# First stage: context loads issued by SP's queue, weights, products and constants by POOL's

## The chip, the cores and the metric

The kernel runs on one core of a Trainium2 chip. The metric is the device time of one execution in microseconds. The engines are PE (matrix products), DVE (VectorE), ACT (ScalarE), POOL (GpSimd) and SP (which here only issues DMAs). A DMA is issued by an engine in its program order: a DMA that has to wait for something holds up all that stands behind it on the same engine. SP's DMAs go through queue q1 (hardware_dynamic), POOL's through q0 (software_dynamic), ACT's few through q10. All three share the core's 16 DMA engines.

## The reference

The input is x (8 x 64 x 512), a context (8 x 1601 x 512) and a mask. Six blocks follow each other, each one added to x after a layer norm. Only the first one matters here; it is a slot attention, repeated three times with the same weights:

```python
Pn = rmsnorm(P, input_norm_w)                 # P: the context
k_proj = Pn @ Wk.T
v_proj = Pn @ Wv.T
for _ in range(NUM_ITERS):                    # 3
    sn = rmsnorm(slots, slot_norm_w)
    q_proj = sn @ Wq.T
    scores = jnp.einsum('bkd,bmd->bkm', q_proj, k_proj) * SCALE
    attn = jax.nn.softmax(scores, axis=-2)
    attn = attn / (jnp.sum(attn, axis=-1, keepdims=True) + EPS)
    updates = jnp.einsum('bkm,bmd->bkd', attn, v_proj)
    slots = gru_cell(updates, slots, gru_wih, gru_whh, gru_bih, gru_bhh)
```

The second block is a state space scan, a product and a feed-forward layer. Its scan is computed as a convolution whose response is a sum over powers of the decay: y_j = sum over n of C B A^j.

## The kernel before

The first stage (about 0 to 802 us) never forms k_proj and v_proj. It multiplies the weights instead: G = Wq^T Wk (`product`, line 489), and Wv with the three input matrices of the recurrent cell (`merged`, line 478). Queries go through G and are then compared with the raw context. G and the three products are stored to HBM once and reloaded in the second and third pass. The products are what the change calls s1.G and s1.m0 to s1.m2.

In each of the three passes the 8 batch rows are done in four pairs. For each pair the contexts of both rows are read anew from HBM, transposed (`transposed`, line 411: 1536 and 1792 KB for the two halves of a row, from rows of 3 and 3.5 KB) and natural (`natural`, line 416: as many bytes, in rows of 2 KB a token that lie behind each other, 12 and 14 KB for row 0 of the pair). A pass moves 54 MB of them. The transposed contexts of a pair go into RA and RB, the natural ones into RC and parts of T and PR; each place is loaded again as soon as the matmuls that read it are done, which is what the waits in `s1_pool` say: `S{h}.{b}` (scores of half h of pair b), `U{h}.{b}` (updates).

After the four pairs comes the recurrent cell with six tiles of weights, whh0, wih0, whh2, wih2, whh1, wih1 in this order (`GRU`, line 391), each 48 matmuls (about 11 us). ACT makes a rounded high part of each tile (`high`), DVE the rest (`low`, line 887), and PE multiplies with both. The tiles come through a ring of 4 slots: SP walks through the list `order` and loads each tile when the one before it in its slot is used (`before[name] + ".used"`), so whh1 waits for whh0 to be used and wih1 for wih0. For the later stages SP goes on with the same list.

POOL issues the context loads of the stage. Then it waits for the last pair's turned updates, issues the load of the mask (line 2064) and computes the powers, 64 dependent multiplications on tiles of 128 x 64 (`s2_pool`, lines 1070 and 1073):

```python
pool.wait_ge(*at.done("s2.decay"))
pool.tensor_tensor(pw[:, 0], abc[:, 1], abc[:, 2], ALU.mult).then_inc(*at.step())
for j in range(1, S):
    pool.wait_ge(*at.own())
    pool.tensor_tensor(pw[:, j], pw[:, j - 1], abc[:, 0], ALU.mult).then_inc(*at.step("s2.powers"))
```

DVE sums them (`response_dve`, line 782) inside the third pass's recurrent cell, after the low parts of the fourth tile (wih2) and ahead of the gate products (L929) and of the low part of the fifth (whh1). ACT makes 48 diagonal tiles of the response (L777) between its tanh and its last sigmoids.

In the first pass there is more: the layer norm of x (L494, L317 on PE), G (L489), the sums of squares of the contexts (L642 on ACT, L801 on DVE), and the merged products (L478).

Of the kernel before, what the change touches and what calls it, by code (L numbers as in the profile page):

```python
# [11 lines left out]
P = 128  # L12
# [12 lines left out]
RING = 4  # L25
# [109 lines left out]

def sem_names():
    return (["tensor_done", "scalar_done", "vector_done", "pool_done", "x_loaded", "consts_loaded", "G_stored", "merged_stored0", "merged_stored1", "merged_stored2", "mask_loaded", "out_stored"]
            + [f"weights_loaded{s}" for s in range(RING)]
            + [f"spare_loaded{s}" for s in range(4)]
            + [f"ctxT_loaded{u}{h}" for u in (0, 1) for h in (0, 1)] + [f"ctxN_loaded{u}{h}" for u in (0, 1) for h in (0, 1)])  # L140


def build(nc, marks, new, t, stages=(1, 2, 3, 4, 5, 6)):
    ctx = ExitStack()
    with ctx:
        address = {}

        def sb(name, shape, dt=FP32):
            address[name] = nc.sbuf_base
            return ctx.enter_context(nc.sbuf_tensor(name, shape, dt))  # L150

        def part(name, of, k=0, n=D):
# [5 lines left out]
        ring = [sb(f"ring{s}", [P, KC, D]) for s in range(RING)]  # L158
        RA, RB, RC = (sb(n, [P, MT * D]) for n in ("RA", "RB", "RC"))
        n0 = HALF[0][1]  # L160
        CT = [RA[:, 0:KC * n0 * P].rearrange("p (c m) -> p c m", c=KC),
              RA[:, KC * n0 * P:KC * MP].rearrange("p (c m) -> p c m", c=KC)]
# [8 lines left out]
        rows = sb("rows", [P, NROW])  # L171
        gw = sb("gw", [P, 2, KC, E_])
# [5 lines left out]
        misc = sb("misc", [P, 512])  # L178
# [24 lines left out]
        scratch = [nc.dram_tensor(f"merged{k}", (P, KC, D), FP32).ap() for k in range(4)]  # L203
# [7 lines left out]
        def row(name, n):  # L211
            return rows[:, RAT[name]:RAT[name] + n]

        sems = {n: ctx.enter_context(nc.semaphore(n)) for n in sem_names()}
        block = ctx.enter_context(nc.Block())

# [6 lines left out]
        order = []  # L223
# [15 lines left out]
        slot, before, place = {}, {}, 0  # L239
# [167 lines left out]
                 [pair(SN, 0), pair(SN, 1), pair(SN, 2), pair(UP, 3)],  # L407
                 [pair(SN, 0), pair(SN, 1), pair(SN, 2), pair(SN, 3)]]

        def s1_pool(pool, at):  # L410
            def transposed(L, b, u, h):
                m0, mt = HALF[h]
                pool.dma_start(CT1[u][h][:, :, :], t["ctxT"][b * 2 + u, :, :, m0 * P:(m0 + mt) * P])\
                    .then_inc(*at.load(f"ctxT_loaded{u}{h}", f"{L}.ct{h}.{u}.{b}"))

            def natural(L, b, u, h):
                m0, mt = HALF[h]
                if u == 0:
                    pool.dma_start(CN0[:, m0:m0 + mt, :], t["ctxN"][b * 2, :, m0:m0 + mt, :])\
                        .then_inc(*at.load(f"ctxN_loaded{u}{h}", f"{L}.cn{h}.{u}.{b}"))  # L420
                    return
                for k, c0, c1 in ((3, 0, 4), (4, 0, 2)) if h == 0 else ((4, 2, 4), (5, 0, 4)):
                    m = 4 * (k - 3)
                    pool.dma_start(TS[k][:, c0:c1, :], t["ctxN"][b * 2 + 1, :, m + c0:m + c1, :])\
                        .then_inc(*at.load(f"ctxN_loaded{u}{h}", f"{L}.cn{h}.{u}.{b}"))
                if h:
                    pool.dma_start(CN1[MT - 1], t["ctxN"][b * 2 + 1, :, MT - 1, :])\
                        .then_inc(*at.load(f"ctxN_loaded{u}{h}", f"{L}.cn{h}.{u}.{b}"))

            for h in (0, 1):  # L430
                for u in (0, 1):
                    natural("s1.0", 0, u, h)
            for h in (0, 1):
                for u in (0, 1):
                    transposed("s1.0", 0, u, h)
            for it in range(3):
                L, N = f"s1.{it}", f"s1.{it + 1}"
                for b in range(PAIRS - 1):
                    for h in (0, 1):
                        pool.wait_ge(*at.done(f"{L}.S{h}.{b}"))  # L440
                        for u in (0, 1):
                            transposed(L, b + 1, u, h)
                    if b:
                        for h in (0, 1):
                            pool.wait_ge(*at.done(f"{L}.U{h}.{b - 1}"))
                            for u in (0, 1):
                                natural(L, b, u, h)
                if it < 2:
                    for h in (0, 1):
                        pool.wait_ge(*at.done(f"{L}.S{h}.{PAIRS - 1}"))  # L450
                        transposed(N, 0, 1, h)
                for h in (0, 1):
                    pool.wait_ge(*at.done(f"{L}.U{h}.{PAIRS - 2}"))
                    for u in (0, 1):
                        natural(L, PAIRS - 1, u, h)
                if it == 2:
                    continue
                for h in (0, 1):
                    pool.wait_ge(*at.done(f"{L}.U{h}.{PAIRS - 1}"))
                    natural(N, 0, 0, h)  # L460
                pool.wait_ge(*at.done(f"{L}.z.3"))
                for h in (0, 1):
                    transposed(N, 0, 0, h)
                pool.wait_ge(*at.done(f"{L}.sl"))
                for h in (0, 1):
                    natural(N, 0, 1, h)

        def s1_pe(pe, at):
            def merged(g):
# [588 lines left out]
        abc = misc[:, 256:448].rearrange("p (a c n) -> p a c n", a=3, c=KC)  # L1058
# [431 lines left out]
        def s4_pool(pool, at):  # L1490
            if 3 in stages:
                pool.wait_ge(*at.done("s3.x5"))
            pool.memset(KT[:, :, n0 * P + M1:MP], 0.0).then_inc(*at.step("s4.pad"))
            for b in range(B):
                N, L = f"s4.{b}", f"s4.{b - 1}"
                m0, mt = HALF[0]
                if b:
                    pool.wait_ge(*at.done(f"{L}.V0"))
                pool.dma_start(CT[0][:, :, :], t["ctxT"][b, :, :, 0:mt * P]).then_inc(*at.load("ctxT_loaded00", f"{N}.ct0"))
                pool.wait_ge(*at.done(f"{N}.ct0"))  # L1500
                if b == 0:
                    pool.wait_ge(*at.done("s4.ln.done"))
                pool.tensor_copy(CH[0][:, :, :], CT[0][:, :, :]).then_inc(*at.step(f"{N}.high0"))
                pool.wait_ge(*at.own())
                pool.tensor_tensor(CL[0][:, :, :], CT[0][:, :, :], CH[0][:, :, :].bitcast(FP32), ALU.subtract).then_inc(*at.step(f"{N}.low0"))

                m0, mt = HALF[1]
                if b:
                    pool.wait_ge(*at.done(f"{L}.t{BLOCKS - 1}"))
                pool.dma_start(CT[1][:, :, :], t["ctxT"][b, :, :, m0 * P:(m0 + mt) * P]).then_inc(*at.load("ctxT_loaded01", f"{N}.ct1"))  # L1510

        def s4_pe(pe, at):
            norm_pe(pe, at, "s4.ln", X, chunk_steps("x3.") if 3 in stages else ["x"])
# [495 lines left out]
        def _(sync):  # L2009
            at = Steps(sems, "out_stored", marks, new)  # L2010

            for dst, src in ((X[:, :, :], t["x"]), (sq[:, :, :], t["squares"]), (vec[:, :], t["vecs"])):
                sync.dma_start(dst, src).then_inc(*at.load("x_loaded", "x"))
            for name, tile in order:
                if tile == "made":
                    for dst, src in ((rows[:, :], t["rows"]), (gw[:, :, :, :], t["gates"]), (misc[:, 256:448].rearrange("p (a b) -> p a b", a=3), t["abc"])):
                        sync.dma_start(dst, src).then_inc(*at.load("consts_loaded", "consts"))
                    at.same("abc", "consts")
                    continue
                if tile is not None:  # L2020
                    if before[name]:
                        sync.wait_ge(*at.done(before[name] + ".used"))
                    if before[name] == "s1.0.G":
                        sync.wait_ge(*at.done("s1.G.stored"))
                    source = t["tiles"][tile] if isinstance(tile, int) else scratch[("s1.G", "s1.m0", "s1.m1", "s1.m2").index(tile)]
                    if not isinstance(tile, int):
                        sync.wait_ge(*at.done(f"{tile}.stored"))
                    sync.dma_start(ring[slot[name]][:, :, :], source).then_inc(*at.load(f"weights_loaded{slot[name]}", name))
                    continue
                if name == "s3.moe":  # L2030
                    for x in before[name]:
# [147 lines left out]
```

## Time and profile before

| | |
|---|---|
| median of 3 runs | 3310.79 us (3310.77 to 3312.28) |
| the profiled execution | 3310.42 us, its span 3308.6 us |
| PE busy | 2950.1 us, 89% |
| DVE, ACT, POOL busy | 1337.6, 1025.8, 268.0 us |
| q1 (SP) | 190.57 MB, 15.2% of 16 engines |
| q0 (POOL) | 192.23 MB, 14.8% |
| DMA share in 0 to 40, 40 to 100, 100 to 200, 200 to 400, 400 to 600, 600 to 800 us | 0.97, 0.86, 0.63, 0.49, 0.72, 0.62 |

The span is what the profiler saw from the first to the last instruction. Busy time is no measure of what a change is worth: what counts is which wait ends last at each place, and the chain of waits shows that.

### The profile page before, as it was taken

How to read it: one execution, taken by the hardware profiler on the slowest of the kernel's cores; microseconds unless marked ns; L12 is line 12 of the kernel's file. 1: busy time of each engine (PE TensorE's matmuls, PEld its weight loads, DVE VectorE, ACT ScalarE, POOL GpSimd, SP SyncE). 2: the span in 40 equal slices, each digit the busy share in tenths (PEclk: the TensorE clock that was granted, in tenths of full speed). 3: DMA queues.
4: the chain of work that ended last, by engine and by line, in shares of the span. 5: the costliest groups of instructions: out<-in, count | busy, mean ns of one | idle time of the engine just before them, and what ended most of it. 6: DMA issues, size and time to landing. Idle time of an engine off the chain costs nothing.

```text
span 3308.6 us, 35885 instructions
## 1 busy us (share of the span) xinstructions
PE 2950.1 (89%) x14622; PEld 2016.9 (61%) x14622; DVE 1337.6 (40%) x2005; ACT 1025.8 (31%) x1717; POOL 268.0 (8%) x274
## 2 busy tenths in 40 slices
PE   7766889888878879999999988999999999988787
PEld 3324537345555347888888857778777877844432
DVE  3435454454842243333333352442443344245211
ACT  3223212224331234433434322422332333233200
POOL 1110120122010000000000002011011101000000
PEclk9887999999889978999999999999999999998899
DMA  8663693861011002222222221001100100021097
GB/s 358 263 241 130 241 412 122 352 267 72 1 52 63 38 13 102 101 93 97 101 89 101 93 78 42 23 20 42 42 23 20 42 23 20 23 108 39 26 419 304
DMA packets 62267, 388.74 MB, mean 117 GB/s; under 512 B 5696, under 2 KB 12096, under 8 KB 32704
## 3 DMA queue, kind: packets, MB, share of 16 engines
q1 hardware_dynamic: 26640, 190.57, 15.2%
q0 software_dynamic: 29024, 192.23, 14.8%
q10 hardware_dynamic: 6480, 4.20, 0.4%
q8 instruction: 91, 1.49, 0.2%
q14 instruction: 32, 0.26, 0.0%
HBM read 381.72 MB, written 5.24 MB: 117 GB/s over the span
## 4 chain that ended last, share of the span: by engine, by line
PE 76%; DVE 7%; DMA 6%; ACT 5%; issue 4%; POOL 2%; SPq 0%; DVEq 0%; POOLq 0%; ACTq 0%
PE PS L373 10%; PE PS L375 10%; PE PS L374 10%; PE PS L544 4%; PE PS L296 4%; PE PS L1571 4%; PE PS L519 3%; PE PS L1552 3%; PE PS L1535 3%; PE PS L1554 3%; PE PS L1553 3%; PE PS L1537 3%; PE PS L1536 3%; DMA PR<-in_ctxN 3%; DMA ring<-in_experts 2%
## 5 line engine op out<-in xcount | busy, mean ns | idle before, releaser
L373 PE MATMUL PS<-X_high,W_high 128*128 128x512 f32 x576 | 226.1, 392 | 27.6 <-POOL W_part L1029 27.6
L374 PE MATMUL PS<-X_low,W_high 128*128 128x512 f32 x576 | 225.6, 392 | 0.0
L375 PE MATMUL PS<-X_high,W_part 128*128 128x512 f32 x576 | 225.5, 391 | 0.0
L375 PE MATMUL PS<-H_high,W_part 128*128 128x512 f32 x576 | 224.4, 390 | 0.0
L374 PE MATMUL PS<-H_low,W_high 128*128 128x512 f32 x576 | 224.4, 390 | 0.0
L373 PE MATMUL PS<-H_high,W_high 128*128 128x512 f32 x576 | 224.4, 390 | 0.0
L1037 DVE TENSOR_TENSOR W_part<-ring,W_high 128x2048 fp32r<-128x2048 f32 x63 | 147.0, 2334 | 188.6 <-ACT W_high L1004 188.6
L1004 ACT ACTIVATE W_high<-ring 128x2048 fp32r<-128x2048 f32 x72 | 136.9, 1914 | 255.0 <-PE PS L375 255.0
L1735 DVE TENSOR_TENSOR RB<-PS,rows 128x512 f32<-128x512 f32 x104 | 71.9, 691 | 307.2 <-PE PS L1554 307.2
L1043 DVE TENSOR_TENSOR H_low<-T,H_high 128x512 fp32r<-128x512 f32 x144 | 99.7, 692 | 221.2 <-ACT H_high L1024 221.2
L1535 PE MATMUL PS<-C_high,W_part 128*128 128x384 f32 (+2 forms) x512 | 177.7, 347 | 4.9 <-DVE W_part L1707 4.9
L1665 ACT ACTIVATE RC<-PS,vec 128x384 f32<-128x384 f32 (+2 forms) x128 | 76.2, 595 | 326.9 <-PE PS L1537 326.9
L1537 PE MATMUL PS<-C_high,W_part 128*128 128x384 f32 (+2 forms) x512 | 176.5, 345 | 0.0
L1536 PE MATMUL PS<-C_low,W_part 128*128 128x384 f32 (+2 forms) x512 | 176.5, 345 | 0.0
L544 PE MATMUL PS<-RC,PTs 128*64 128x512 f32 x312 | 144.7, 622 | 31.1 <-DVE PTs L871 23.4
L1552 PE MATMUL PS<-W_part,C_high 128*128 128x512 f32 x416 | 164.9, 396 | 0.0
L1553 PE MATMUL PS<-W_part,C_high 128*128 128x512 f32 x416 | 162.3, 390 | 0.0
L1554 PE MATMUL PS<-W_part,C_low 128*128 128x512 f32 x416 | 162.3, 390 | 0.0
L519 PE MATMUL PS<-RA,PR 128*64 128x448 f32 (+1 forms) x384 | 145.3, 538 | 18.5 <-DMA RB<-in_ctxT 8.2
L1023 ACT ACTIVATE T<-PS,vec 128x512 f32<-128x512 f32 x144 | 99.2, 689 | 197.1 <-PE PS L375 187.4
L296 PE MATMUL PS<-T,ring 128*128 128x512 f32 x288 | 135.4, 633 | 20.9 <-DVE T L363 10.0
L519 PE MATMUL PS<-RB,PR 128*64 128x448 f32 (+1 forms) x384 | 145.5, 539 | 0.0
(314 smaller groups left out, 5804.4 us busy)
## 6 DMA issues: line engine op xcount, KB each, us to landing
ring<-in_experts SPq DMA_DIRECT2D x96, 1024.0 KB, 4.8
ring<-in_tiles SPq DMA_DIRECT2D x39, 1024.0 KB, 4.8
RA<-in_ctxT POOLq DMA_DIRECT2D x20, 1792.0 KB, 8.9
RA<-in_ctxT POOLq DMA_DIRECT2D x20, 1536.0 KB, 6.9
T<-in_ctxN POOLq DMA_DIRECT2D x24, 1024.0 KB, 13.7
RA<-in_experts SPq DMA_DIRECT2D x24, 1024.0 KB, 12.4
RC<-in_ctxN POOLq DMA_DIRECT2D x12, 1792.0 KB, 12.7
RB<-in_ctxT POOLq DMA_DIRECT2D x12, 1792.0 KB, 13.4
```

The source lines that it names most:

```text
L296: mm = pe.matmul(bank(k), wt(w)[:, c, oc * P:(oc + 1) * P], x[:, c, :], start=(a == 0 and c == 0), stop=(a == len(terms) - 1 and c == KC - 1))
L373: pe.matmul(ps, a, xh, start=start, stop=False)
L374: pe.matmul(ps, a, xl, start=False, stop=False)
L375: return pe.matmul(ps, b, xh, start=False, stop=stop)
L519: mm = pe.matmul(PS[u * S:(u + 1) * S, 2 * h + j, 0:w], QP[:, c, u * S:(u + 1) * S], CT1[u][h][:, c, j * w:(j + 1) * w], start=(c == 0), s ...
L544: mm = pe.matmul(PS[u * S:(u + 1) * S, 6, :], A_[:, m, u * S:(u + 1) * S], cn(u, m), start=(m == 0), stop=(m == MT - 1))
L1535: pe.matmul(bank(n % 4, w), wkh[:, c, f], CH[h][:, c, m], start=(c == 0), stop=False)
L1536: pe.matmul(bank(n % 4, w), wkh[:, c, f], CL[h][:, c, m], start=False, stop=False)
L1537: mm = pe.matmul(bank(n % 4, w), wkl[:, c, f], CH[h][:, c, m], start=False, stop=(c == KC - 1))
L1552: pe.matmul(bank(k), CH[h][:, c, m], wvh[:, c, :], start=(c == 0), stop=False)
L1553: pe.matmul(bank(k), CH[h][:, c, m], wvl[:, c, :], start=False, stop=False)
L1554: mm = pe.matmul(bank(k), CL[h][:, c, m], wvh[:, c, :], start=False, stop=(c == KC - 1))
```

## The change

In the first stage the two issuers change places. The context loads, all with the same waits in the same order, are issued by SP, after x, squares and vecs. The weight tiles, the reloads of G and of the merged products, and the three constants (rows, gates, abc) are issued by POOL, in the list's order and with the same waits. POOL's wait for the turned updates, the mask and the powers stand behind them. The later stages' tiles are still SP's, behind the context loads. Semaphores get names of their own, so that each has one issuer; this also renames two in the fourth stage.

```diff
-        def s1_pool(pool, at):
+        def s1_loads(pool, at):
             def transposed(L, b, u, h):
...
+        def s1_pool(pool, at):
+            for name, tile in order:
+                if tile == "made":
+                    for dst, src in ((rows[:, :], t["rows"]), (gw[:, :, :, :], t["gates"]), (misc[:, 256:448].rearrange("p (a b) -> p a b", a=3), t["abc"])):
+                        pool.dma_start(dst, src).then_inc(*at.load("consts_loaded", "consts"))
+                    at.same("abc", "consts")
+                    continue
+                if not name.startswith("s1."):
+                    continue
+                if before[name]:
+                    pool.wait_ge(*at.done(before[name] + ".used"))
+                if before[name] == "s1.0.G":
+                    pool.wait_ge(*at.done("s1.G.stored"))
+                source = t["tiles"][tile] if isinstance(tile, int) else scratch[("s1.G", "s1.m0", "s1.m1", "s1.m2").index(tile)]
+                if not isinstance(tile, int):
+                    pool.wait_ge(*at.done(f"{tile}.stored"))
+                pool.dma_start(ring[slot[name]][:, :, :], source).then_inc(*at.load(f"recurrent_loaded{slot[name]}", name))
...
             for dst, src in ((X[:, :, :], t["x"]), (sq[:, :, :], t["squares"]), (vec[:, :], t["vecs"])):
                 sync.dma_start(dst, src).then_inc(*at.load("x_loaded", "x"))
+            if 1 in stages:
+                s1_loads(sync, at)
             for name, tile in order:
-                if tile == "made":
-                    for dst, src in ((rows[:, :], t["rows"]), (gw[:, :, :, :], t["gates"]), (misc[:, 256:448].rearrange("p (a b) -> p a b", a=3), t["abc"])):
-                        sync.dma_start(dst, src).then_inc(*at.load("consts_loaded", "consts"))
-                    at.same("abc", "consts")
+                if name.startswith("s1."):
                     continue
                 if tile is not None:
                     if before[name]:
                         sync.wait_ge(*at.done(before[name] + ".used"))
-                    if before[name] == "s1.0.G":
-                        sync.wait_ge(*at.done("s1.G.stored"))
-                    source = t["tiles"][tile] if isinstance(tile, int) else scratch[("s1.G", "s1.m0", "s1.m1", "s1.m2").index(tile)]
-                    if not isinstance(tile, int):
-                        sync.wait_ge(*at.done(f"{tile}.stored"))
-                    sync.dma_start(ring[slot[name]][:, :, :], source).then_inc(*at.load(f"weights_loaded{slot[name]}", name))
+                    sync.dma_start(ring[slot[name]][:, :, :], t["tiles"][tile]).then_inc(*at.load(f"weights_loaded{slot[name]}", name))
                     continue
```

## Rows read from the trace of the kernel before

**Rows 1.** Chain of waits, 0 to 800 us: start, length, engine or DMA, line.
```profile
35.11 6.87 PE PS L489 x16
...
66.41 0.74 POOL RA L413
67.14 9.97 DMA RB<-in_ctxT
...
86.82 6.23 PE PS L519 x32
...
120.16 11.33 DMA PR<-in_ctxN
...
674.38 23.54 DMA PR<-in_ctxN
...
733.99 0.53 POOL PR L2064
...
765.70 4.43 DVE kconv L782
```

**Rows 2.** Timeline of PE at the start: start, length, operation, [idle before, releaser].
```profile
13.20 5.59 PE L494 MATMUL PS<-X,sq 128*128 128x512 f32 x8
22.87 8.80 PE L489 MATMUL PS<-ring 128*128 128x512 f32 x16 [4.08 <-DMA ring<-in_tiles]
```

**Rows 3.** Windows: length, busy of PE, PEld, DVE, ACT, POOL; clock, DMA share, GB/s.
```profile
22.80:31.60 8.80, 8.73 (x17) 3.82 (x18) 0.00 (x0) 0.69 (x1) 0.00 (x0) 0.81 1.02 416
...
710.40:716.70 6.30, 0.00 (x0) 0.00 (x0) 6.13 (x8) 4.58 (x6) 0.00 (x0) 0.50 0.74 307
716.80:720.40 3.60, 3.60 (x10) 1.12 (x12) 3.46 (x5) 1.95 (x2) 0.00 (x0) 0.53 0.00 0
```

**Rows 4.** DMA: POOL's queue to 5.6, both from 5.6 to 12.8; two issues.
```profile
q0 software_dynamic: 9, 0.11, 4.6%
...
q0 software_dynamic: 244, 2.36, 77.7%
q1 hardware_dynamic: 261, 0.65, 22.9%
...
RB<-in_ctxT POOLq DMA_DIRECT2D x1, 1792.0 KB, 51.7
...
vec<-in_vecs SPq DMA_DIRECT2D x1, 149.0 KB, 11.0
```

**Rows 5.** Timeline of SP's queue: the third pass's last tile, wih1.
```profile
753.05 0.32 SPq L2028 DMA_DIRECT2D ring<-merged  x1
```

**Rows 6.** Timeline of POOL: the first of the 64 powers.
```profile
734.64 0.32 POOL L1070 TENSOR_TENSOR RC<-misc 128x64 f32<-128x64 f32 x1
```

**Rows 7.** Chain of waits, 733 to 776 us: three of the powers.
```profile
755.72 2.35 POOL RC L1073
...
764.95 0.33 POOL RC L1073
...
765.35 0.33 POOL RC L1073
```

**Rows 8.** Timeline of DVE in the third pass's recurrent cell.
```profile
755.59 2.29 DVE L887 TENSOR_TENSOR W_part<-ring,G_high 128x2048 fp32r<-128x2048 f32 x1 [9.33 <-ACT G_high L725]
...
773.00 2.28 DVE L887 TENSOR_TENSOR W_part<-ring,G_high 128x2048 fp32r<-128x2048 f32 x1
```

**Rows 9.** Timeline of ACT: the diagonals of the response.
```profile
779.47 14.16 ACT L777 ACTIVATE RB<-sq,kconv 128x128 f32<-128x128 f32 x48
```

**Rows 10.** DMA: two lone loads; packets and rate, 630 to 695 (POOL's), 3145 to 3270 (SP's).
```profile
ring<-in_tiles SPq DMA_DIRECT2D x1, 1024.0 KB, 4.7
...
PR<-in_mask POOLq DMA_DIRECT2D x1, 832.0 KB, 4.8
...
DMA packets 3959, 26.84 MB, mean 413 GB/s; under 512 B 331, under 2 KB 331, under 8 KB 2944
...
DMA packets 7234, 52.72 MB, mean 422 GB/s; under 512 B 800, under 2 KB 800, under 8 KB 800
```

More of the change, by code:

```diff
@@ L137, in sem_names @@
     return (["tensor_done", "scalar_done", "vector_done", "pool_done", "x_loaded", "consts_loaded", "G_stored", "merged_stored0", "merged_stored1", "merged_stored2", "mask_loaded", "out_stored"]
-            + [f"weights_loaded{s}" for s in range(RING)]
+            + [f"weights_loaded{s}" for s in range(RING)] + [f"recurrent_loaded{s}" for s in range(RING)] + ["half_loaded0", "half_loaded1"]
             + [f"spare_loaded{s}" for s in range(4)]
@@ L1498, in s4_pool @@
                     pool.wait_ge(*at.done(f"{L}.V0"))
-                pool.dma_start(CT[0][:, :, :], t["ctxT"][b, :, :, 0:mt * P]).then_inc(*at.load("ctxT_loaded00", f"{N}.ct0"))
+                pool.dma_start(CT[0][:, :, :], t["ctxT"][b, :, :, 0:mt * P]).then_inc(*at.load("half_loaded0", f"{N}.ct0"))
                 pool.wait_ge(*at.done(f"{N}.ct0"))
@@ L1509, in s4_pool @@
                     pool.wait_ge(*at.done(f"{L}.t{BLOCKS - 1}"))
-                pool.dma_start(CT[1][:, :, :], t["ctxT"][b, :, :, m0 * P:(m0 + mt) * P]).then_inc(*at.load("ctxT_loaded01", f"{N}.ct1"))
+                pool.dma_start(CT[1][:, :, :], t["ctxT"][b, :, :, m0 * P:(m0 + mt) * P]).then_inc(*at.load("half_loaded1", f"{N}.ct1"))
         def s4_pe(pe, at):
```

## The prediction, made before the result was known

> **What bounds the kernel now.** I read first the chain of waits over the first stage (0 to 800 us), since the change touches only who issues that stage's DMAs. Three places in it hang on this. At the start PE waits for the first two weight tiles until 22.87 [rows 2]. In each pass PE waits for context loads: for a pair's transposed contexts (67.14, 9.97 us) and for its natural ones (120.16, 11.33 us, much the same for the next pairs; 23.54 us from 674.38 in the last pass). And near the end the chain leaves PE, runs over POOL's mask load and the powers of stage 2, to VectorE's reduction at 765.70 [rows 1]. Then I read PE's start (its own wait at 22.87 is only 4.08 us, since the mean's matmuls fill 13.20 to 18.8) [rows 2], the granted clock around idle stretches [rows 3], the DMA rows of the start [rows 4], and the four engines between 730 and 800 us [rows 5 to 9]. Last, what the two kinds of queue do alone and when full [rows 10].
>
> **The late powers: the loss.** SP loses its weight loads, so POOL gets them in SP's order, each with its wait. The last two of the third pass wait until whh0 and wih0 are used; SP issued the last of them, wih1, at 753.05 [rows 5]. POOL runs its instructions in order, and behind this wait now stand the mask load and all 64 steps of the powers, which before began at 734.64, right after the mask load of 733.99 (0.53 us to issue) [rows 6]. Now: the wait ends at 753.05, the tile's issue takes 0.53 (the mask's row; it is of nearly the same size), the mask 0.65 to the first power: start at 754.2, 19.6 us late.
>
> The powers then run quicker. Two steps in a row start 0.40 us apart (764.95 and 765.35), so 64 steps are 25.7 us; they took 31.1 (734.64 to 765.70). The excess is two long steps of one pattern, 2.3 us at 744.18 and 2.35 us at 755.72, each on top of a VectorE subtraction of a weight tile (the second one is at 755.59), and three steps at 735 to 738 of 0.66 to 0.87, beside VectorE's update_low [rows 7, 8]. In the new position only the subtraction at 755.59 meets them, since VectorE has nothing after it but the wait for the powers: 25.7 + 2.0 = 27.7, end at 781.9. That is 16.2 us later than 765.70. Bounds: 14.2 (nothing meets them) and 19.6 (as long as before).
>
> Who waits: VectorE stands at the reduction (L782), and behind it are the reset-gate products and the low part of whh1, which began at 773.00 and ended at 775.28 [rows 8]. PE's step whh1 began at 775.3, with no slack. So PE stands idle from 775.3 to 791.5, and the whole 16.2 us are on the path. After such an idle the clock is low: at 710.4 to 716.7 PE idled, and the next 3.6 us ran at 0.53, the lower of the two levels [rows 3]; half of 3.6 is 1.8 us lost (bounds 0 and 1.9, the loss at 22.87, below). Behind that ScalarE's 48 diagonals (14.16 us at 779.47) [rows 9] move with the response, and PE's last 22.5 us move with them, so the end of the stage moves by 16.2 + 1.8 = **18.0 us**. No later stage gives it back: its first work needs x1.
>
> On the page SBUF — State Buffer (section on its port rule) the Trainium skill says that a VectorE instruction with two SBUF inputs holds up a GpSimd instruction that reads SBUF for its whole length. The trace agrees: a power of 0.33 us takes 2.35 [rows 7, 8]. By it the saving is that of the rows.
>
> **The start: a gain.** SP's queue has x, squares and vecs (1.66 MB) first, in both kernels. Before, POOL's queue moved contexts against them: 0.11 MB until 5.6, then 244 packets with 2.36 MB, while SP's moved 261 packets with 0.65 MB [rows 4]. The packets of both queues are about equal in number, so they alternate, and the small packets of squares and vecs (3.5 and 1.2 KB a row) pay for the size of the other's: 12 KB rows of contexts. Now the other's are 8 KB rows of wq. The last 0.41 MB of SP's three took 5.6 to 12.7; the pair of packets shrinks by (8+3.5)/(12+3.5) = 0.74 and (8+1.2)/(12+1.2) = 0.70, so 7.1 us become 5.2, and vecs land at 10.8. PE's first matmul comes 1.9 us earlier (bounds: 0 and 3).
>
> wq and wk (2.1 MB) sit at the head of POOL's queue: from 5.6 to 10.8 it moves 5.2 x 0.415 (MB a us, as full queues do) - 0.41 = 1.7 MB, the rest by about 13. The mean ends at 18.8 - 1.9 = 16.9, and the products follow without a wait: 16.9 for 22.87, 6.0 us. Without the idle before them the clock doesn't drop: the first two products took 8.80 us at a mean clock of 0.81, the next two, as many, 6.87 [rows 1 to 3]; 1.9 more. Sum 7.9.
>
> Does the DMA side follow? All loads of the first 59 us are the same bytes, the engines are full until then, and before the last transposed context landed at 7.33 + 51.7 = 59.0 [rows 4]. wih1, issued before when the q products end (59.2), now comes at 51 and takes part, so the last context lands at about 61. The scores that need it would start at 65.9 - 7.9 = 58.0: a stall of 3 us. But the chain before went over the second pair's contexts, released at 66.4 and landed at 77.1 [rows 1], PE idle for 5 us. Now they are released at 58.2, queue behind the last one, and 3.15 MB at 0.413 MB a us are in by 69.5. Both halves (6.8 MB) are in at 61 + 16.6 = 78, where PE started the second half at 86.8. So the stall falls into the old idle time, and **8.6 us** are won (bounds 4, if vecs come no sooner and the clock doesn't care, and 9.5).
>
> **The context loads: a small gain.** A lone 1024 KB load of SP landed in 4.7 us and a lone 832 KB one of POOL in 4.8. Less their bytes at 0.415 (2.5 and 2.05) that is 2.2 and 2.75: 0.5 us of a load's delay, for SP. Full, POOL's queue made 413 GB/s and SP's 422 (other packets: 8 KB only) [rows 10]. While the engines are full a quicker start is worth nothing, so it counts once a link: three natural loads in the first pass, two links in each of the two others. 7 x 0.4 = **2.8 us**. Bounds: 0, and 7 x 0.9 + 2.2% of the 240 us in which the chain waits on full queues = 11.5. I take the small end, as the rate's difference has another cause at hand (packet size), which goes with the data and not with the queue.
>
> The Trainium skill, page DMA: Bandwidth & Descriptors (section on latency), gives about 1 us to the first byte for GpSimd's path and 0.6 for SP's. By it the term is 2.8, the same; the rows carry it.
>
> **Edits at nothing.** Weights by POOL: each of the tiles of a pass is issued two steps (22 us) ahead of its use, and a slower issue of 0.2 to 0.5 us is hidden by that; without this cover it would be 0.5 a tile. Consts behind wk: needed by VectorE at 60, in by about 20. SP has nothing else in the stage that its context waits could hold up: s2.out's load waits for whh2 in any case (764). Renamed semaphores of stage 4: nothing.
>
> **Sum.** The profiled execution's own time is 3310.4 (span 3308.6), 0.4 below the median of 3310.8. 3310.4 + 18.0 - 8.6 - 2.8 = **3317.0 us**.
>
> **The rivals.**
> 1. The start gives only a little: vecs land no sooner, or the last contexts, behind everything of SP, hold the scores. For it: these contexts land at 59 already. Against: 5 us of idle at 72 to 77 to take it up. Then 8.6 becomes 2: 3323.6. Chance 0.13.
> 2. (other side) SP's queue carries contexts faster, at the full 422 against 413 and 0.9 us sooner: 18.0 - 8.6 - 11.5 = -2.1: 3308.3. It decides the sign from 9.4 us of gain on the context loads upward. For it: the landings; against: POOL's queue is full to 0.99 in the waits, so no engine starves on it. On the page SBUF — State Buffer the skill has a rule that speaks for this one, that VectorE's work can keep GpSimd from writing descriptors; full queues show no such hole here. Chance 0.15.
> 3. SP's queue carries them worse: the trace has none of SP's loads with rows of 3 KB out of a larger row. If it costs 3% of 240 us: 3324. Chance 0.12.
> 4. The powers aren't late: POOL finds its waits over earlier than SP's rows say, or PE has slack that I don't see. Then only the gains are left: 3299. Against: L782 stands in the chain. Chance 0.05.
> 5. My forecast, 3312 to 3321: 0.55.
>
> **How the numbers follow.** A measurement of this kernel tells 0.2%, 6.6 us, from no change, that is from 3304.2 to 3317.4. My forecast lies near the upper bound: half of its 0.55 is slower, half the same. Slower: 0.27 + 0.13 + 0.11 = 0.51; faster: 0.05 and a fifth of the second rival = 0.08; same: 0.41. Range 3306 to 3325: it leaves out the fourth case and the tails of the others.
>
> **What would show it.** Right: the first power at 754 less the shift of the stage so far (some 11), so near 743; PE idle for 16 us just before whh1, released by VectorE, which waits for POOL; the first product at 17; the second pair's scores some 8 us earlier; context waits as long as before less half a microsecond. Wrong: no such idle; the first product still at 22; DMA waits that change by microseconds each.

## The result, and the profile after

The changed kernel takes 3328.16 us (median of 5, 3326.31 to 3329.82), the kernel before 3310.79 in the same series: 17.4 us slower by the two medians. The ratio with its 95% interval is 1.0049 (1.0036 to 1.0062). I had forecast 3317.0 us, range 3306 to 3325. The sign was right, the size was not: 17.4 us against 6.2 (3317.0 less 3310.8), and outside the range. The profiled execution grew by 16.2 us (span 3308.6 to 3324.8), and that is what the two traces can explain.

The chain of waits of the changed kernel, 0 to 840 us (start, length, engine or DMA, line; most line numbers of the products and of VectorE's work are 18 higher than before):

```profile
1.67 10.10 DMA vec<-in_vecs
12.46 5.21 PE PS L512 x8
17.66 6.87 PE PS L507 x16
...
53.57 5.38 PE PS L537 x32
58.95 2.94 issue
61.89 6.23 PE PS L537 x32
71.02 5.31 PE PS L537 x32
76.33 4.19 issue
80.52 7.92 PE PS L537 x32
88.44 13.93 PE PS L496 x32
...
115.05 11.37 DMA PR<-in_ctxN
...
237.19 17.85 DMA PR<-in_ctxN
...
383.77 10.32 DMA RB<-in_ctxT
...
669.29 22.90 DMA PR<-in_ctxN
...
776.84 4.43 DVE kconv L800
812.26 2.51 DVE T L967 x4
815.63 6.47 PE PS L329 x8
...
832.27 6.68 PE PS L329 x8
```

Set beside the rows of before, each place gives the shift so far. The first product starts at 17.66 for 22.87, 5.2 us sooner. The first pair's scores start 7.2 sooner (60.72 before), the second half of the second pair's 6.3 (80.52 for 86.82), what follows it 4.6 (88.44 for 93.05). The last natural contexts of the first pass land 4.1 us sooner, those of the third pass 5.7 (692.2 for 697.9) [rows 1]. (In the first pass the wait that ends there was, before, `242.70 16.48 DMA PR<-in_ctxN`.) Then the sign turns: the response is reduced at 776.84 for 765.70, 11.1 late, the state is done 13.0 late (812.26 for 799.24), and after the two layer norms of the next stage it is 15.0.

POOL and then DVE in the third pass's recurrent cell, from the timelines of the two engines (start, length, operation, what ended the idle time before it):

```profile
748.02 0.53 POOL L484 DMA_DIRECT2D ring<-merged  x1 [10.62 <-PE PS L375]
748.54 0.53 POOL L2076 DMA_DIRECT2D PR<-in_mask  x1
749.20 0.32 POOL L1088 TENSOR_TENSOR RC<-misc 128x64 f32<-128x64 f32 x1
749.60 27.21 POOL L1091 TENSOR_TENSOR RC<-RC,misc 128x64 f32<-128x64 f32 x63
```
```profile
776.84 4.42 DVE L800 TENSOR_REDUCE kconv<-RC 128x256 f32<-128x4096 f32 x1 [24.27 <-POOL RC L1091]
784.14 2.28 DVE L905 TENSOR_TENSOR W_part<-ring,G_high 128x2048 fp32r<-128x2048 f32 x1
```

The load of wih1 stands in front of the mask and the powers. These begin at 749.20, 14.6 us later than before, on a stage that is 5.0 us ahead (wih1's load is issued at 748.02 for 753.05): 19.6 later in the stage's own time, as worked out. They take 27.6 us for 31.1. PE's waits, 720 to 900 us (waiting line, releaser, total, times, longest):

```profile
PE PS L373 <- DVE W_part L905: 16.7, 1, 16.7
```

Before, this wait was 0.2 us.

### The profile page after: what moved, and what is told of

It is laid out like the page before. It is cut to its first block, busy times and chain, and to the rows that moved or that the text cites. A ratio compares the mean times of both kernels' runs of the same rounds, so it can differ in the third digit from the quotient of the medians.

```text
span 3324.8 us, 35873 instructions
## 1 busy us (share of the span) xinstructions
PE 2953.9 (89%) x14622; PEld 2016.8 (61%) x14622; DVE 1336.4 (40%) x2005; ACT 1027.0 (31%) x1717; POOL 199.6 (6%) x171
## 2 busy tenths in 40 slices
DMA packets 75115, 388.74 MB, mean 117 GB/s; under 512 B 5568, under 2 KB 11856, under 8 KB 45552
## 4 chain that ended last, share of the span: by engine, by line
PE 77%; DVE 7%; DMA 6%; ACT 5%; issue 4%; POOL 1%; SPq 0%; DVEq 0%; POOLq 0%; ACTq 0%
PE PS L373 10%; PE PS L375 10%; PE PS L374 10%; PE PS L562 4%; PE PS L296 4%; PE PS L537 4%; PE PS L1589 3%; PE PS L1570 3%; PE PS L1553 3%; PE PS L1571 3%; PE PS L1572 3%; PE PS L1554 3%; PE PS L1555 3%; DMA PR<-in_ctxN 3%; DMA ring<-in_experts 2%
## 5 line engine op out<-in xcount | busy, mean ns | idle before, releaser
L373 PE MATMUL PS<-X_high,W_high 128*128 128x512 f32 x576 | 225.8, 392 | 27.6 <-POOL W_part L1047 27.6
L537 PE MATMUL PS<-RA,PR 128*64 128x448 f32 (+1 forms) x384 | 146.4, 541 | 20.3 <-issue 11.2
## 6 DMA issues: line engine op xcount, KB each, us to landing
RA<-in_experts SPq DMA_DIRECT2D x24, 1024.0 KB, 13.1
RC<-in_ctxN SPq DMA_DIRECT2D x12, 1536.0 KB, 10.6
```

Source lines behind the costliest of these rows:

```text
L373: pe.matmul(ps, a, xh, start=start, stop=False)
L537: mm = pe.matmul(PS[u * S:(u + 1) * S, 2 * h + j, 0:w], QP[:, c, u * S:(u + 1) * S], CT1[u][h][:, c, j * w:(j + 1) * w], start=(c == 0), s ...
```

## The experiments

Each ran in a series beside the kernel before on one chip. In those series the kernel before was at 3311.9 to 3312.5 us, so ratios are compared, each with its 95% interval.

**1. The last two tiles back to SP** (e1), and everything else of the change kept:

```diff
+        LATE = ("s1.2.whh1", "s1.2.wih1")
...
-                if not name.startswith("s1."):
+                if not name.startswith("s1.") or name in LATE:
...
-                if name.startswith("s1."):
+                if name.startswith("s1.") and name not in LATE:
...
```

> The changed kernel, but the third pass's last two weight tiles (whh1, wih1) are issued by SP again, so that POOL has the mask and the powers before it as in the kernel before. My theory: the late powers cost 18.0 us at the end of the first stage and nothing else of the change costs anything; the 2.3 us that the layer norms behind it lost to a low clock are chance of phase and may go too. Then 3328.2 - 18.0 = 3310 (3306 to 3312), PE's idle before whh1 falls from 16.7 us to under 1, and the whole stays some 5 us ahead of the kernel before at the end of the third pass's updates. Rival: the swap of queues itself costs, in the context loads by SP's queue or in the clock, and the powers' delay only hides part of it: 3316 or more.

Measured: 3306.0 us, ratio 0.9981 (0.9972 to 0.9990), 6.5 us faster than the kernel before. The response is reduced at 755.28, and PE's wait before whh1 is gone (PE's waits):

```profile
PE PS L373 <- DVE W_part L907: 0.3, 1, 0.3
```

So the order on POOL is the whole loss, and without it the change is a gain. The rival (3316 or more) is out.

**2. A smaller dose** (e2): POOL does the mask and the powers ahead of wih1's load, but still behind that of whh1.

```diff
+                if name == "s1.2.wih1":
+                    pool.wait_ge(*at.done("s1.2.UT.3"))
+                    pool.dma_start(PR[:, 0, :].bitcast(I32), t["mask"]).then_inc(*at.load("mask_loaded", "mask"))
+                    s2_powers(pool, at)
                 if before[name]:
...
-                pool.wait_ge(*at.done("s1.2.UT.3"))
-            pool.dma_start(PR[:, 0, :].bitcast(I32), t["mask"]).then_inc(*at.load("mask_loaded", "mask"))
```

> The changed kernel, but POOL does the mask load and the powers between the loads of whh1 and wih1 of the third pass: they wait for whh0 to be used, not for wih0. A smaller dose of the same delay. My theory: the powers start one step (11.1 us) sooner, but meet two of VectorE's weight subtractions again in place of one (2 us): end 9 us sooner, PE idles for 7 to 8 us in place of 16.7, and the clock still falls: 3328.2 - 9 = 3319 (3316 to 3321). wih1 itself, loaded some 17 us later, is still in before its step. Rival (a step in program order is free as long as PE has other work, the cost is the clock's alone): under 3314 or no change from 3328.

Measured: 3317.25 us, ratio 1.0010 (1.0001 to 1.0019). The idle before whh1 is 7.5 us, and the powers take 29.6 us with two of DVE's subtractions in their way (timelines of POOL and of DVE, then PE's waits):

```profile
740.54 29.19 POOL L1095 TENSOR_TENSOR RC<-RC,misc 128x64 f32<-128x64 f32 x63
```
```profile
769.76 4.42 DVE L804 TENSOR_REDUCE kconv<-RC 128x256 f32<-128x4096 f32 x1 [15.09 <-POOL RC L1095]
```
```profile
PE PS L373 <- DVE W_part L909: 7.5, 1, 7.5
```

The wait goes with the dose: 0.3, 7.5, 16.7 us of idle for ratios of 0.9981, 1.0010 and 1.0046 to 1.0049.

**3. The start alone** (e3): from the kernel before, the first loads' issuers swapped and all later ones left.

```diff
+            s1_contexts(sync, at, True)
...
-                s1_pool(pool, at)
+                s1_tiles(pool, at, "first_loaded")
+                s1_contexts(pool, at, False)
```

> The kernel before, with the issuers of the first loads alone swapped: POOL issues wq, wk, the constants, wv, wih0, wih2 and wih1 of the first pass, SP the first pair's contexts; all later loads as before. My theory: all of the gain is made here, 4.6 to 5 us, of which 0.9 by the earlier vecs, 4.1 by wq and wk, 1.9 by the clock, less the stall of the scores for the last context: 3310.8 - 4.8 = 3306 (3304 to 3308). Rival: the gain needs SP's quicker issue of the later contexts too: 3309 or more.

Measured: 3307.19 us, ratio 0.9985 (0.9976 to 0.9994), 5.0 us. The start's gain stands by itself. Experiment 1 has the later loads swapped as well, and its ratio is 0.0004 lower (1.3 us), which is within the intervals.

**4. The later contexts alone** (e4): the start as before, SP issues the later contexts, POOL the tiles of the passes but for the last two.

```diff
-                s1_loads(sync, at)
+                s1_tiles(sync, at, "first_loaded", lambda name: name in FIRST)
+                s1_contexts(sync, at, False)
```

> The kernel before at its start (SP issues the tiles, POOL the first pair's contexts), the changed kernel after it, with the last two tiles of the third pass by SP: what is left of the change is that SP issues the later contexts. My theory: next to nothing, since a context load by SP starts 0.2 us sooner for the natural ones and 0.3 later for the transposed ones, whose packets are halves: 3310.8 - 0.8 (3308.5 to 3311.5). The forecast said 2.8 less: 3308. Rival: SP's queue is worse with rows of 3 KB: 3313 or more.

Measured: 3312.67 us beside 3312.49, ratio 0.9999 (0.9990 to 1.0008). The medians show no gain, but the interval reaches from 3.3 us faster to 2.6 us slower: it excludes neither the forecast's 2.8 us nor the 1.1 us by which the traces' shift grew between 93 and 698 us. For the single loads the traces say more. Here is the first wait of the second pass, in this run and then before (row by row: the end of PE's scores, which frees the place, and RB's load):

```profile
383.33 5.41 PE PS L546 x32
389.34 10.19 DMA RB<-in_ctxT
```
```profile
382.29 5.40 PE PS L519 x32
389.44 9.39 DMA RB<-in_ctxT
```

RB's load took longer, but it was issued 0.6 us after the scores' end, and before 1.75 us after it. From the end of the scores to the landing it is 10.8 us for 11.1.

**5. The first contexts ahead of everything** (e5): e1, and POOL's wih0, wih2 and wih1 of the first pass wait for the second pair's contexts.

```diff
+                if name == "s1.wih0":
+                    pool.wait_ge(*at.done("s1.0.ct1.1.1"))
                 if before[name]:
```

> e1_last_two_by_sp, and POOL's next tiles of the first pass (wih0, wih2, wih1, 3.1 MB) wait until the second pair's transposed contexts have landed. This takes away what I take for the reason that the start won 4.6 us and not 8.6: in the changed kernel the last context of the first pair comes 2.94 us late, so the next half's contexts are asked for late, the DMA engines run empty for 2 us, and PE waits 4.2 us more. My theory: no stall at 59, the second pair's second half starts at 77.5 for 80.5, three microseconds less than e1 through to the end: 3306.0 - 3 = 3303. Rival (the shortfall is the clock's or the issue's by SP): the same time as e1, 3306.

Measured: 3306.23 us, ratio 0.9984 (0.9975 to 0.9993), e1's time. The forecast fell. The stall is gone (the first pair's scores run through, 64 matmuls in 11.42 us), but the second pair's second half is in at 79.8, not at 77.5, and the tile that I had held back comes only at 88.9 (chain of waits of e5, three pieces of it; then GB/s in 40 slices of 50 to 80 us):

```profile
54.19 11.42 PE PS L541 x64
66.20 13.60 DMA RB<-in_ctxT
80.09 8.71 DMA ring<-in_tiles
```
```profile
GB/s 401 397 315 43 29 5 0 0 0 0 0 0 0 0 66 119 377 418 410 418 422 410 414 401 410 396 406 406 401 406 411 401 406 416 397 408 416 311 100 147
```

The experiment is not a clean test of the stall, though, because it adds a wait of its own. PE did the second half's scores from 79.89 to 86.1 at a clock of 1.00; in e1 they began at 80.54, took 8.50 us and ended at 89.0. So at this point e5 was 2.9 us ahead. Then PE stood idle for 2.8 us for the held tile (timeline of PE), and the merged product after it took 15.57 us where e1's took 13.93:

```profile
88.94 2.04 PE L500 MATMUL PS<-ring 128*128 128x512 f32 x2 [2.81 <-DMA ring<-in_tiles]
```

The held tile took back what the missing stall had won.

The row of rates shows why the contexts came no sooner than 79.8. SP issues the next contexts at 59.6 (first scores done), and full rate comes only at 62: 6.8 MB then need until 79.8. From that release to the last landing it took 20.2 us here, 20.3 in the next experiment and 20.4 before (66.4 to 86.8) [rows 1]; in the changed kernel, with the stall in it, 21.5.

**6. The first weights ahead of the contexts** (e7): e5, and SP issues x, squares, vecs, wq, wk and then contexts; POOL's constants and wv wait for wk.

```diff
+            pool.wait_ge(*at.done("s1.wk"))
...
+            for name in LATE[:2]:
+                sync.dma_start(ring[slot[name]][:, :, :], t["tiles"][AT[name]]).then_inc(*at.load(f"weights_loaded{slot[name]}", name))
             if 1 in stages:
                 s1_loads(sync, at)
```

(with wq and wk put at the head of LATE.)

> e5_contexts_first, and wq and wk are issued by SP behind x, squares and vecs and ahead of the contexts; POOL's constants and wv wait for wk to land, so nothing shares the engines with what PE needs first. My theory: vecs land at 7.5 for 11.5, the first product starts at 13 for 17.5, the last context of the first pair lands at 53 for 59, and the second pair's second half starts at 70 to 72 for 77.5: 5 to 7 us less than e5: 3297 (3294 to 3300). Rival (the DMA engines are full until 59 whatever the order, and this is what sets the second pair): the first product is earlier, but the time is e5's.

Measured: 3301.56 us, ratio 0.9966 (0.9954 to 0.9978). Its first product starts at 14.23, and the second pair is in at 75.8, not at 70 to 72: again 20.3 us after its release at 55.5. Run once more beside the next one:

> e7_weights_ahead_of_contexts beside e8 in one series: 3301.6 (3300 to 3304).

3304.43 us, ratio 0.9975 (0.9966 to 0.9984): less of a gain than the first time, within the intervals.

**7. One tile in between** (e8): e7, but wih0 waits only for the first pair.

```diff
-                if name == "s1.wih0":
-                    pool.wait_ge(*at.done("s1.0.ct1.1.1"))
+                if name in ("s1.wih0", "s1.wih2"):
+                    pool.wait_ge(*at.done("s1.0.ct1.1.0" if name == "s1.wih0" else "s1.0.ct1.1.1"))
```

> e7_weights_ahead_of_contexts, but the first of the three held tiles, wih0, waits only for the first pair's last context and falls into the time in which the DMA engines are empty (53 to 57 us); wih2 and wih1 wait for the second pair's as before. In e7 PE waited for wih0 until 85.3 though the second pair's scores were done at 82.2. My theory: the merged product starts at 82 to 83, 3 us sooner, and all behind it: 3 us less than e7, 3298.5 (3296 to 3301). Rival: wih0 delays the second pair's contexts by as much as it comes sooner: e7's time, 3301.5.

Measured: 3303.03 us, ratio 0.9966 (0.9955 to 0.9978), not to be told from e7. There was less to win than I had expected: PE's wait for wih0 was 0.4 us in the first trace of e7, where the scores ended at 84.9 and not at 82.2, and 1.7 us in the second. The rival had it: PE no longer waits for wih0, but the second pair's contexts come later (PE starts on the second half at 77.68, where they were in at 74.4 in the other), and the merged product starts at 83.92 against 84.09 in the run of e7 beside it (chain of waits, of e8, then of e7's second run):

```profile
77.68 6.23 PE PS L542 x32
83.92 13.93 PE PS L501 x32
```
```profile
74.69 9.27 DMA ring<-in_tiles
84.09 13.97 PE PS L501 x32
```

**8. The changed kernel once more**, in one series with e5 and e7.

> The changed kernel itself, beside the others on one chip: 1.0049 of the kernel before (1.004 to 1.006), so that the differences to the experiments are of one series. The late powers' whole cost, this less e1's, should be 20 us: 16.2 of waiting, 1.8 of low clock right behind it, and 2 in the layer norms of the next stage.

Measured: 3327.73 us, ratio 1.0046 (1.0032 to 1.0060). Less e1's 0.9981 that is 0.0065 of 3312, 21.5 us, where the traces' account gives 20; the two intervals together leave about 5 us to either side.

The best versions are e7 and e8, 8 to 11 us faster than the kernel before in their series; e1 is the changed kernel with its one fault mended.

## Why the prediction was right in sign and wrong in size

**The late powers: right, nearly to the tenth.** Start 19.6 us late in the stage's own time (measured 19.6), duration 27.7 (27.6), idle of PE 16.2 (16.7), low clock behind it 1.8 (the shift grows by 1.9, from 11.1 at the reduction to 13.0 at the state), and 18.0 us from the third pass to the state (from 5.0 ahead to 13.0 behind: 18.0). Experiments 1 and 2 show the cause and its dose.

**Missing: 2 us of clock in the next stage.** I had written that no later stage gives the loss back; I hadn't asked whether one adds to it. The mean's matmuls of the two layer norms took 6.47 and 6.68 us, where they took 5.14 and 6.01 before. In the three traces with a long idle before whh1 (both of the changed kernel, and e2) they take 6.2 to 6.5 and 6.5 to 6.7, in the eight without 5.1 to 5.4 and 6.0 to 6.2. The granted clock of a stretch of each, in the columns of [rows 3], the changed kernel and then the kernel before, 830 to 860 us:

```profile
830.00:860.00 30.00, 17.10 (x27) 7.36 (x28) 21.23 (x34) 3.11 (x5) 0.00 (x0) 0.72 0.00 0
```
```profile
830.00:860.00 30.00, 21.78 (x70) 14.31 (x71) 29.82 (x58) 8.15 (x27) 0.00 (x0) 0.83 0.00 1
```

The stretches are not the same work, so what they show is a level of the clock, not its cause. That the earlier idle brings it about is a correlation over eleven executions; I ran nothing that changes the clock alone.

**The start: the step that failed.** Forecast 8.6 us, measured 4.6 in the trace and 5.0 in experiment 3. The step is "so the stall falls into the old idle time": it took the second pair's loads to follow the first pair's on full DMA engines, and put at nothing the delay with which a load starts. By its own terms:

- The first matmul came 0.9 us sooner (12.78 to 11.90), not 1.9. The queues' packets alternate, as I had worked out: 256 of POOL's and 263 of SP's between 5.6 and 11.9 us (DMA rows of that window). What I mis-sized is the packets. I took the other queue's at 12 KB before and 8 KB after, but the rows have them at 9.7 KB (2.36 MB in 244) [rows 4] and 7.7 KB, and SP's at 2.5 and 2.9 KB. So a pair shrinks from 12.2 to 10.6 KB, to 0.87 and not to 0.74 or 0.70: 7.2 us become 6.3, which is the measured 5.6 to 11.9.

```profile
q0 software_dynamic: 256, 1.97, 73.8%
q1 hardware_dynamic: 263, 0.76, 29.9%
```

- wq and wk were in time, and the clock held through the products (6.87 us for 8.80), as forecast.
- The last context of the first pair was late as forecast (61.9, a stall of 2.94 us), but I had all contexts of the second pair in at 78, which holds only if the DMA engines stay full from the first pair over to the second. They did not: the second half is asked for when the scores of the first pair's second half are done, at 68.15, the rate of the loads before it falls away at 68.5, and full rate is back only at 71 (GB/s in 40 slices of 61 to 81 us, the changed kernel):

```profile
GB/s 254 387 412 406 393 436 418 412 399 436 418 412 393 393 399 191 47 122 115 308 423 411 409 409 409 423 423 409 423 423 416 416 394 416 416 401 386 385 418 412
```

Two and a half microseconds of low rate, in the slices from 68.5 to 71, and the half starts at 80.52. (Two sums of the working are off besides: 3.15 MB behind 61 are in by 68.6, not 69.5, and 86.8 less 78 is 8.8, not 8.6. Neither makes the difference.) So 6.3 us were left of the 7.2 at 53.57.
- And 1.7 of these went to the clock: PE stood idle for 4.19 us before that half, where it had been 2.4 before, and the same 32 matmuls took 7.92 us at a mean clock of 0.78, where they took 6.23 at 1.00 (windows of the changed kernel, then of the kernel before):

```profile
80.50:88.40 7.90, 7.88 (x33) 3.08 (x33) 4.58 (x6) 0.00 (x0) 0.00 (x0) 0.78 0.87 337
```
```profile
86.80:93.00 6.20, 6.18 (x33) 2.67 (x33) 2.63 (x2) 0.00 (x0) 0.00 (x0) 1.00 0.97 391
```

I had counted the clock where an idle goes away and behind the powers, not where one grows. Experiment 5 shows the same from the other side: without the stall the second half began only 0.7 us sooner than in e1 but ran at full clock, and was done 2.9 us sooner, until the held tile took that back.

**The later context loads: forecast 2.8 us, 1.1 in the trace; experiment 4 can't tell.** Counted from the end of the matmuls that free a place to the last landing, SP's loads are indeed quicker: the first and second of the first pass 12.7 for 13.2 and 12.8 for 13.1 us, the transposed one of the second pass 10.9 for 11.1, the natural ones of the second and third pass 24.7 for 25.1 and 24.5 for 25.4. About a quarter of a microsecond of each comes before the DMA: PE's matmuls end, and SP issues 0.02 us later, POOL 0.28. The exception is the first pass's last wait, 19.2 for 18.3 us. There a term failed that I had put at nothing, the weights by POOL ("a slower issue of 0.2 to 0.5 us is hidden by that"). Four tiles are asked for 11 us ahead of that wait, and within it their queue still had 1.29 MB to move, where it had 0.79 before (DMA rows from 235.8 to 255.1 of the changed kernel, its queue of tiles; then from 240.8 to 259.2 of the kernel before):

```profile
q0 software_dynamic: 189, 1.29, 16.0%
```
```profile
q1 hardware_dynamic: 112, 0.79, 10.1%
```

Half a megabyte more is 1.2 us at 0.41 MB a us, an estimate beside the 0.9 us measured. Experiment 3 (tiles by SP) has 18.6 us and 0.71 MB there, experiment 4 (tiles by POOL) 19.2 and 1.27. The six waits together are 1.5 us of gain. How that becomes the 1.1 of the shift is not accounted for; clock losses differ between the two traces in the same stretch.

The Trainium skill, page DMA: Bandwidth & Descriptors (section on latency), has the first byte of SP's path 0.4 us sooner and names no shape. For rows of 3 KB the trace does not show it: from the first issue of a half to its last landing it is 10.9 us by either queue (383.18 to 394.09, and 387.98 to 398.83 before), and the measurement decides. The bound "SP's queue carries them worse" did not come true.

**The sum** in the trace: 18.0 + 2.0 - 4.6 - 1.1 = 14.3, of the 15.0 measured behind the layer norms, and 1.2 more in all of the rest: 16.2. (The 0.7 between 14.3 and 15.0 were lost ahead of the powers, 0.5 of them in the last updates of the third pass: 13.53 us for 13.06.) The forecast was 18.0 - 8.6 - 2.8 = 6.6. Of the 9.6 us between, 4.0 are the start, 1.7 the context loads, 2.0 the layer norms' clock, and 1.9 are spread over the rest and not accounted for. Of the rivals, the third (3324) and the first (3323.6) were the nearest in number. The third's mechanism is not what the runs show. The first's is in part: the last contexts did hold the scores, though the start still gave 4.6 us and not 2.

## What to carry to other kernels

Before a DMA is moved to another engine's queue, list what stands behind it there, and for each what its wait now waits for: one load that waits for a late buffer held 64 small multiplications for 19.6 us, and these stood on a path with no slack. A gain at the start is worth what it is at the next place where a load is asked for by the work itself; follow it to there, with the load's start and not only its bytes. And where an idle time grows, add the clock behind it, and look at the next stage's clock too.

## What I had not expected of the hardware

SP's queue took the first contexts at once and then held SP at the issue of the next (timeline of SP, the changed kernel):

```profile
6.37 1.33 SPq L413 DMA_DIRECT2D RA<-in_ctxT  x1
7.74 14.84 SPq L413 DMA_DIRECT2D RB<-in_ctxT  x1
22.61 7.97 SPq L413 DMA_DIRECT2D RA<-in_ctxT  x1
30.63 3.56 SPq L413 DMA_DIRECT2D RB<-in_ctxT  x1
```

An issue that takes 0.3 to 0.6 us elsewhere took 14.84. POOL had issued the same eleven loads in 7 us before. The rows show no cost of it here, as SP had nothing else to do; a load with a short deadline behind such a row of loads would have waited.

Over SP's queue the transposed contexts went as twice as many packets, 3.2 KB each where POOL's had 6.2 (DMA rows of the kernel before, 65 to 90 us, then of the changed kernel, 61 to 81):

```profile
q0 software_dynamic: 1300, 8.12, 85.0%
```
```profile
q1 hardware_dynamic: 2325, 7.47, 96.9%
```

The whole kernel has 75115 packets for the same 388.74 MB, the kernel before 62267. Where this queue has the DMA engines to itself, the rows show no difference of rate: 406 to 423 GB/s in most slices above.

The times of one kernel on one chip spread over up to 9 us (e1: 3300.84 to 3309.39), with the mean granted clock from 0.951 to 0.948. One source of it shows in the traces: behind the same idle some executions lose the clock and some do not. In the second pass PE stood idle for 3.3 us before 28 update matmuls in both traces of the changed kernel, and these took 7.93 us in one and 6.23 in the other (chain of waits, first the profiled execution of the result, then that of experiment 8):

```profile
471.97 7.93 PE PS L562 x28
```
```profile
473.91 6.23 PE PS L562 x28
```
